# Two cross-attention layers on one core: a shorter lag between the layers, a moved wait, four idle places

## The reference

```python
# layer 0
q, k_t, v_t = x @ W_q, text @ W_k, text @ W_v            # split into 20 heads
probs_t = softmax(q k_t^T / 4)
text_out = probs_t v_t
qsem = l2norm(probs_t @ text)                            # 20 heads x 512 columns
fused = q k_ip^T / 4 + 0.5 * qsem @ l2norm(ip)^T
ip_out = (softmax(fused) * spatial_mask) v_ip
x = (text_out + ip_out) @ W_out + b_out + x
# layer 1
q, k, v, k_ip, v_ip = x @ Wq.T, text @ Wk.T, text @ Wv.T, ip @ Wk_ip.T, ip @ Wv_ip.T
out = softmax(q k^T / 4) v + softmax(q k_ip^T / 4) v_ip
x = out @ Wo.T + bo + x
```

## Time and profile before

| | us |
|---|---|
| median of 3 runs | 3416.84 (3412.73 to 3419.73) |
| the profiled execution, its time | 3415.48 |
| its span, first to last instruction | 3413.3 |
| TensorE busy in the span | 3339.5 (98%) |
| VectorE, ScalarE, GpSimd busy | 1977.4, 1824.1, 1070.4 |
| mean granted TensorE clock | 0.994 of full speed |

### The profile page before, as it was taken

The page is one execution under the profiler, slowest core; times in us unless marked ns, Lnnn a source line. Parts: engine busy times, 40 slices in busy tenths (PEclk is TensorE's granted clock), DMA queues, the critical chain, the costliest instruction groups (busy, mean ns, idle before and its releaser), DMA issues.

```text
span 3413.3 us, 65707 instructions
## 1 busy us (share of the span) xinstructions
PE 3339.5 (98%) x24736; PEld 2889.3 (85%) x24736; DVE 1977.4 (58%) x5493; ACT 1824.1 (53%) x3983; POOL 1070.4 (31%) x918
## 2 busy tenths in 40 slices
PE   6999999999999999999999999999999999999989
PEld 4888988887888888888888888888888898998855
DVE  5444455556556565565656556665565556556566
ACT  2333333455555555555655556555565556565667
POOL 3111011334332333333333232333423322322357
PEclk8999999999999999999999999999999999999999
DMA  6433824233358322233357432323336532222232
GB/s 191 120 77 69 94 54 101 72 98 87 81 72 104 78 69 71 73 96 84 87 72 76 95 73 69 79 71 106 86 73 75 66 59 49 62 51 53 46 83 57
DMA packets 648781, 271.28 MB, mean 79 GB/s; under 512 B 479666, under 2 KB 599426, under 8 KB 648468
## 3 DMA queue, kind: packets, MB, share of 16 engines
q1 hardware_dynamic: 646356, 267.06, 38.3%
q10 hardware_dynamic: 2112, 0.03, 0.0%
HBM read 187.97 MB, written 79.04 MB: 78 GB/s over the span
## 4 chain that ended last, share of the span: by engine, by line
PE 91%; DVE 4%; ACT 2%; POOL 1%; DMA 1%; issue 1%; SPq 0%; POOLq 0%; DVEq 0%; ACTq 0%
PE acc L1182 9%; PE acc L1175 9%; PE acc L1178 8%; PE acc L1177 8%; PE acc L1183 8%; PE acc L1176 7%; PE score L1142 4%; PE score L1233 4%; PE spare L1233 4%; PE score L1144 4%; PE av L1220 4%; PE av L1224 4%; PE spare L1274 2%; PE spare L1323 2%; PE score L1274 2%; PE score L1323 2%
## 5 line engine op out<-in xcount | busy, mean ns | idle before, releaser
L1413 ACT ACTIVATE prob<-score 128x512 f32<-128x512 f32 x1188 | 710.1, 598 | 1174.3 <-PE score L1144 1170.4
L1854 POOL TENSOR_TENSOR prob_lo<-prob,prob_hi 128x512 fp32r<-128x512 f32 x609 | 791.0, 1300 | 1489.5 <-ACT prob_hi L1416 1488.9
L1175 PE MATMUL acc<-tok_v,prob_hi 128*128 128x300 f32 x2240 | 907.9, 405 | 2.0 <-ACT prob_hi L1416 2.0
L1177 PE MATMUL acc<-tok_lo,prob_hi 128*128 128x256 f32 (+1 forms) x2560 | 759.9, 297 | 0.0
L1182 PE MATMUL acc<-tok_v,prob_lo 128*128 128x278 f32 (+1 forms) x2560 | 745.4, 291 | 0.0
L1178 PE MATMUL acc<-tok_lo,prob_hi 128*128 128x256 f32 (+1 forms) x2560 | 719.0, 281 | 0.0
L1183 PE MATMUL acc<-tok_v,prob_lo 128*128 128x256 f32 (+1 forms) x2560 | 717.8, 280 | 0.0
L1416 ACT ACTIVATE prob_hi<-score 128x512 fp32r<-128x512 f32 x1188 | 707.1, 595 | 0.0
L1176 PE MATMUL acc<-tok_v,prob_hi 128*128 128x256 f32 x2240 | 627.6, 280 | 0.0
L1178 PEld LDWEIGHTS acc<-tok_lo,prob_hi 128*128 128x128 f32 (+1 forms) x2560 | 483.6, 189 | 8.6 <-issue 2.3
L1177 PEld LDWEIGHTS acc<-tok_lo,prob_hi 128*128 128x128 f32 (+1 forms) x2560 | 484.4, 189 | 5.4 <-issue 3.0
(11 more groups left out here) (341 smaller groups left out, 5007.2 us busy)
## 6 DMA issues: line engine op xcount, KB each, us to landing
k_ring<-k_scr SPq DMA_DIRECT2D x160, 384.0 KB
tok_v<-v_scr SPq DMA_DIRECT2D x158, 176.0 KB, 3.3
v_ring<-v_scr SPq DMA_DIRECT2D x160, 148.5 KB, 3.4
ctx_t<-in_ctxT SPq DMA_DIRECT2D x16, 1024.0 KB, 8.9
q_ring<-q_scr SPq DMA_DIRECT2D x160, 96.0 KB
v_scr<-v_stage SPq DMA_DIRECT2D x28, 440.0 KB, 2.6
v_scr<-v_stage SPq DMA_DIRECT2D x36, 330.0 KB, 9.7
tok_stage<-in_ctx SPq DMA_DIRECT2D x28, 256.0 KB, 3.0
```

The lines of the kernel that those rows point to most:

```text
L1175: e.matmul(out_a[:, 0:SEG + VCOLS], p_hi, tok_v[0:kk, c, seg, v_lo:v_lo + SEG + VCOLS], start=first, stop=False)
L1177: e.matmul(out_a[:, t0:t0 + SEG], p_hi, tok_lo[0:kk, c, seg * SEG:(seg + 1) * SEG], start=False, stop=False)
L1413: e.activation(prob[:, es, :], bank_s[:, :], ACT.Exp, scale=SCALE)
L1854: e.tensor_tensor(prob_lo[:, ps, :], prob[:, es, :], prob_hi.bitcast(F32)[:, ps, :], ALU.subtract).then_inc(s_low[1], 1)
```

## The change

`LAG_UNITS` goes from 124 to 116. The first load of each layer-1 unit stands no earlier than 18 places ahead of its first group, for unit 8 13 places, for unit 15 12 as before. Four idle places (a place taken by a job that does nothing) stand between `x_split` and the q products of units 8 to 14. VectorE's L1604 waits for GpSimd's `v_hi` of two blocks earlier (`s_v3`), which frees the buffer of `v_f`, and no longer for the store of the stage; that wait (`stage_free`) goes to `v_hi`.

```diff
-LAG_UNITS = 124
+LAG_UNITS = 116
...
+LOAD_AHEAD = {B: 13, LAST: 12}
...
-        return first + second + [lambda: None, x_split, Pause(1)] + q
+        return first + second + [lambda: None, x_split, Pause(1)] + ([] if u == LAST else [lambda: None] * 4) + q
...
-            load_at.setdefault(max(at, start_of[place[(u, 0)]] - (12 if u == LAST else 14)) if u in (B, LAST) else at, []).append(g)
+            load_at.setdefault(max(at, start_of[place[(u, 0)]] - LOAD_AHEAD.get(u, 18)) if u >= B else at, []).append(g)
...
                     e.wait_ge(s_bg, job[key] + 1)
-                    stage_free(e, i)
-                    if i < NT + 2:
-                        e.wait_ge(s_first_v, 2 * (i - 1))
+                    e.wait_ge(s_v3, i - 1)
                     e.tensor_scalar(f[:, 0:n], bank[bank_of[key]][0:w, 0:n], one[0:w, 0:1], None, ALU.mult).then_inc(s_free, 1)
...
                     e.wait_ge(*out_of_psum[job[key]])
-                    if u == 0:
-                        stage_free(e, i)
-                        if i >= 4:
-                            e.wait_ge(s_first_v, 2 * (i - 3))
-                        else:
-                            e.wait_ge(s_mem, 6)
-                            e.wait_ge(s_more, 1)
+                    stage_free(e, i)
+                    if u == 0 and i < 4:
+                        e.wait_ge(s_mem, 6)
+                        e.wait_ge(s_more, 1)
+                    elif i < NT + 2:
+                        e.wait_ge(s_first_v, 2 * (i - 3 if i < NT else i - 1))
```

## The result

The kernel is slower. After the change it takes 3445.62 us (median of 4 runs, 3442.52 to 3451.03), the kernel before in the same comparison 3417.99 (3412.73 to 3419.73): ratio 1.0085, with a 95% interval of 1.0073 to 1.0097. The profiled execution took 3444.71 us, its span is 3442.9.

What follows compares the result with a forecast made beforehand. TensorE, busy 98%, was taken as the bound, with about 27 us lost in the tail's first 129 us. Tail -11.5, woven side +7.5 and packed maxima +1.0 gave -3.0 us: 3413.8 us, range 3402 to 3425.

Steps and rivals of the forecast that it cites:

- The tail side: Tail: with the lag shorter by 8, one group of unit 14 and its maxima go, 11.5 us shorter.
- Rival C: Tail: unit 15's load, with 0.6 us to spare, comes too late and TensorE waits; 3421 us, chance 0.11.
- Rival B: Tail's first stretch closes up, a third of its 27 us loss going; 3405 us, chance 0.28.
- the woven side: Woven phase: 8 layer-1 steps moved in from the tail cost 0.94 us each, +7.5 us.
- Loads no earlier than 18 ahead: Units 9 to 14: later first loads pack the maxima closer; 1 us, bounds 0 and 8.5.
- Rival D: Packed maxima make six units, and units 8 and 15, wait, 17 us together; 3430 us, chance 0.09.
- Unit 8 and the lead: Lead: unit 8's q must be made 8 steps sooner; cost 0, bound above by one wait of 1.41 us.
- The idle places: Between `x_split` and q products of units 8 to 14: nothing to gain, and other jobs getting closer costs 0.
- The wait of the values: VectorE's L1604 never waited for the stage's store, so moving that wait to `v_hi` is worth 0.
- The prediction's own test: Forecast wrong if woven waits grow over 8 us, unit 15's first maxima wait over 3.4 us, or tail `max_rows` waits go.

Runs made afterwards that it cites:

- kernel with moved loads: Kernel after, with only the two loads for unit 12 issued behind the value load of group 55, not just ahead of unit 10's first query load: 3446.20 us.
- kernel with both collisions removed: Kernel after, with unit 12's loads issued behind the value load of group 55 and two value stores behind the last token fetch: 3428.63 us, ratio 1.0033.
- kernel with added stores: Kernel before, with two added 330 KB stores to an unread buffer, behind token fetch 3 of batches 2 and 3: 3425.69 us, ratio 1.0027.

## Why the prediction was wrong

Forecast 3413.8 us and "same", measured 3445.6; 20 us above the range. No rival named the mechanism.

**The tail side was right in the main.** 10.2 us less against 11.5. The tail's whole steps have 116 matmuls, 4 each, so they are 29, as forecast, and the loads of unit 15 go out ahead of the third store of q. SyncE's queue of the kernel after:

```profile
3306.69 1.43 SPq L1952 DMA_DIRECT2D q_scr<-part_bf  x3
3309.49 0.28 SPq L1987 DMA_DIRECT2D k_ring<-row_scr  x1
...
3313.14 1.96 SPq L1952 DMA_DIRECT2D q_scr<-part_bf  x3
```

Rival C (the load of unit 15 late) did not come: no wait for a DMA in the tail. Rival B didn't either: the stretch that lost 27 us still has a clock of 0.91 against 0.92 before.

**The 7.5 us of the woven side were a fair term, of the wrong sum.** 8 pairs cost some 8.7 us by their matmuls, and a window without jobs, `prob` alone, gives 71.80 / 16 = 4.49 us a pair, forecast 4.44:

```profile
3014.30:3086.10 71.80, 0.00 (x0) 0.00 (x0) 10.93 (x16) 19.12 (x33) 20.83 (x16) 1.00 0.25 56
```

**The step that failed** is that what a change of order does to the DMA queue was priced at nothing. The shifted timetable was taken as 0, at two places of the prediction: "The projections that had stood among the 8 lead steps are still done; they have TensorE time of their own in any phase", and for the idle places "the loss is that other jobs get closer: 0". The first is true of TensorE and says nothing of SyncE. With jobs go their loads and stores, and these are issued in the order of the list on a queue that layer 0's fetches and layer 1's ring loads share. At a third place, "Loads no earlier than 18 ahead", the term of 1 us counted the maxima that come closer together, and not that the load itself comes closer to its reader: 11.7 to 16 us in the kernel after for the units without a wait, 18.1 to 22.4 before. What the runs showed in place of all three: 39.8 us where 8.5 were forecast, 31.3 us more. Of them 15.4 are the three long waits and 7.9 their half-speed stretches. Taking the collisions away gives 17 us back, giving the idle places no weight 13 us; a store among the fetches of the old timetable costs 4 us each. In the list with the weightless places none of the three collisions stands, so both repairs take away the same waits; no run has both.

**Loads no earlier than 18 ahead: 1 us in the prediction, bounds 0 and 8.5.** By itself the rule costs 17 us, twice the upper bound. The place was wrong too: I priced waits of the maxima of six units in the woven phase, and some 13 us lie in the lead. Rival D named this part and its sum (17 us), but by another mechanism; that the sums agree is luck. In the whole change less of it is left: idle time up to 600 us grows by 3.4 us and 3.4 us run at half speed, 5.1 us together. The cost of 0 under "Unit 8 and the lead", with its bound of 1.41 us, was too low by that.

**The idle places: gain nothing in units 8 to 14.** True of the kernel before, from whose trace it was read, and false of lag 116: there five waits of 2.1 us for `x_in_lo` come, 10.6 us with the lag alone and 3.5 us with the rest of the change, and the places take them away. The earlier trace rows could not show it, since the q products stood elsewhere.

**The wait of the values: 0** was right, twice: undone, it changes 1.5 us, inside the spread, and the line's idle time ends by TensorE alone. "Either way the same DMA" is what the kernel with moved loads showed, where `v_hi` waited 5.47 us for it.

The prediction's own test was set well: it was to be wrong "if waits in the woven phase (now 21 us) grow by more than 8 us". They grew by 15.4.

**What stays open.** Even without the collisions found, lag 116 and 120 are 11 to 21 us slower than 124. Of the kernel with both collisions removed the sum is known: its tail begins 25.4 us later than before, 10.6 of idle time (35.1 against 24.5), 8.7 of matmuls, 3.4 of low clock, 2.7 not accounted for; and ends 11.4 us shorter. Nor is it shown what the closer projections of the lead cost by themselves, the largest part of the rule's 17 us. Whether a list exists in which lag 116 wins its 11 us of tail against 9 us of pairs isn't known; none of the kernels run beats the one before.

## What to carry to other kernels

In a kernel whose engines follow one hand-made order, a change to a lag, a due time or a job's weight is first of all a change of what stands next to what on the DMA queue. Before costing steps, list for both orders how far each load stands from its first reader and what is issued ahead of it. 23 of the 40 us lost ahead of the tail were at three such loads: one had come close to its reader (22.4 to 6.5 us) and behind 2.6 MB, two had got a store of small pieces ahead of them. For the first, neither a distance of 9.2 us nor the bytes alone made a wait. A placeholder that the planner counts as work is not free, and one with no weight can serve as well. And when a wait is taken away in such a list, measure the sum: here two repairs gave 0 and 4 us alone and 17 together.

## What the runs showed of the hardware

A store of 330 KB in pieces of 132 bytes took 8.6 to 11.4 us to land where it came alone, and up to 16.5 us where such stores followed one another 5 to 9 us apart (kernel with moved loads). A fetch of 256 KB issued behind one took 7.1 us instead of 3.0, and in the kernel with moved loads 8.5 and 8.7. The same store cost nothing where no near reader stood behind it. A copy of 2.6 MB in long rows ahead of a load with 22.4 us of room cost nothing, loads of 2.6 MB ahead of one with 6.5 us of room a wait of 6.2 us.

Of TensorE's clock: at the waits of 4.2 to 6.3 us looked at here, the granted clock was at the lower level of 1.2 GHz for 3.4 to 6.8 us. At the three waits of the kernel after and the two of the kernel with added stores that cost 1.7 to 2.9 us, a third to two thirds of the wait again. Of the five waits of 2.1 us for `x_in_lo` in the kernel with the lag alone, three have a stretch of 3.4 us behind them; at the waits of up to 1.3 us in the woven phase of the kernel before the clock stayed at 2.4 GHz. The Trainium skill, page "TensorE: Matmul & The Clock Gate", section "What's actually happening", calls the low level the default, which activity releases. The trace agrees: the clock fell at the waits and was back at 2.4 GHz after 3.4 to 6.8 us, with TensorE at work again.
